# A graph layer's aggregation: one four-pass float32 product replaced by two float32r products over a split operand

## The chip, the cores and the metric

The kernel runs on one core of one Trainium2 chip. The metric is the device time of one execution in microseconds. The change is judged by the median of several runs of the changed kernel against the median of the kernel before: 936.79 us, from three runs between 936.75 and 937.58 us.

## The reference

One layer over 1250 nodes with 512 features and 20000 edges: a graph convolution, a linear attention and a two-of-four mixture of delta-rule memories. What the change touches is the graph convolution:

```python
def _L0_gnn_ref(x, W, b, edge_index):
    src = jnp.concatenate([edge_index[0], self_loops])
    dst = jnp.concatenate([edge_index[1], self_loops])
    deg = jax.ops.segment_sum(ones, dst, num_segments=N)
    dinv_sqrt = jnp.where(deg > 0, jax.lax.rsqrt(deg), 0.0)
    norm = dinv_sqrt[src] * dinv_sqrt[dst]
    h = x @ W
    msgs = h[src] * norm[:, None]
    agg = jax.ops.segment_sum(msgs, dst, num_segments=N)
    return jax.nn.relu(agg + b)
...
xn = _layernorm(x, axis=-1)
x = x + _L0_gnn_ref(xn, ...) + _L0_mix_ref(xn[None], ...)[0]
x = x + _L0_ffn_ref(_layernorm(x, axis=-1)[None], ...)[0]
```

## The kernel before, in words

Nodes are tiled by P = 125 rows, so there are NT = 10 tiles of source nodes (s) and 10 of destination nodes (t). The features are 512 = KC * 128 columns.

The kernel is a hand-ordered program: each engine has its own instruction list and they meet only at semaphores. Its stages, in time:

1. Up to about 216 us: layer norm of x, the linear attention, and a sort of the edges into bins by their source tile.
2. Up to about 307 us: the counting. The number of edges from each source node to each destination is built as a product of one-hot matrices (float16) on TensorE (L557), with VectorE making the one-hots (L1646, L1652). ScalarE copies the counts from PSUM into `big`, seen as `cnt` (L1088), and GpSimd adds the self loops (L1337). Between these products TensorE computes h = xn @ W (L690), which ScalarE copies to `hs` (L1084).
3. About 307 to 323 us: TensorE forms the last attention outputs with `mix(7)`, `mix(8)`, `mix(9)` (L571) and the degrees (L719). VectorE adds 1 to the degrees (L1714). A branch, not taken with these inputs, holds further rounds of counting for a bin that overflows (TensorE L724, VectorE L1717). GpSimd takes the power -0.5 of the degrees into `dinv` (L1339). VectorE adds the attention outputs to x (`mix_out`, L1609) and multiplies each `hs` tile by `dinv` in place (L1732).
4. About 323 to 419 us: the aggregation. For each destination tile t TensorE sums ten products `cnt[:, s, t] x hs[:, s]` over s into one PSUM bank (L770), both operands float32. Behind t = 8 and 9, and woven into them, stand token logits (L743) and the first feature projections (L754), and behind t = 5, 6, 8 and 9 transposes of normalised rows (L529). VectorE scales each result by `dinv` and adds the bias (L1740), applies the relu and adds to x (L1743), and takes the statistics of the next layer norm (L1471 to L1476); GpSimd takes the power -0.5 of the variances (L1307); VectorE normalises rows (L1484).
5. From 419 us: the mixture: gates, projections (L754), scatter of rows to DRAM by GpSimd (L1357), ten units of a chunked recurrence up to about 870 us, gather, gate, output projection (L1023).

The order around the change. TensorE runs t = 0 to 9 strictly in order; in t = 0 it waits before each s for `hs_done` (L769), and from t = 2 on it waits for the sum of t - 2 on VectorE (L766). VectorE makes all ten `hs` tiles, with `mix_out(9)` between tiles 3 and 4, before it turns to the sums. SP issues the loads of the five mixture weights once `mix(9)` is done (L415 to L418).

Of the kernel before, what the change touches and what calls it, by code (L numbers as in the profile page):

```python
# [25 lines left out]
P = 125  # L26
NT = N // P
# [71 lines left out]
def gps_layer(nc, d, out):  # L99
    f32, i32, f16, bf16 = mybir.dt.float32, mybir.dt.int32, mybir.dt.float16, mybir.dt.bfloat16  # L100
    ALU = mybir.AluOpType
# [3 lines left out]
    with ctx:  # L105
# [16 lines left out]
        xT = sb("xT", [128, KC, N + 3])  # L122

        big = sb("big", [128, NT * N])
        cnt = big[0:P, :].rearrange("p (t n) -> p t n", t=NT)
        fT = big[:, 0:2 * D].rearrange("p (k n) -> p k n", k=2)
        hs = sb("hs", [P, NT, D])
        W = sb("W", [128, 5, KC, D])
# [23 lines left out]
        xn = sb("xn", [128, 2, D])  # L152
        tA = sb("tA", [128, 2, D])
        tB = sb("tB", [128, 2, D])
        tC = sb("tC", [128, 2, D])
# [4 lines left out]
        b_q1 = sb("b_q1", [128, 2, KC])  # L160
        dinv = sb("dinv", [P, NT])
        deg = sb("deg", [P, NT])
# [196 lines left out]
        def sort_after_q(u):  # L359

            return SORT_KV * (NT - SORT_FROM) + SB * min(2 * u, 8 + u)

        def last_sum(dve, V, t):
            dve.wait_ge(S["y_psum"], t + 1)
            if t >= 2:
                dve.wait_ge(out_stored[t % 2], 32 * (t // 2))
            V.tensor_tensor(tC[0:P, t % 2, :], bank[0:P, 6 + t % 2, :], x_all[:, t, :], ALU.add).then_inc(S["y_done"], 1)
# [3 lines left out]
        def _(sp):  # L371
# [40 lines left out]
            for s in range(NT):  # L412
                sp.wait_ge(S["count_done"], 2 * s + 2)
                sp.dma_start(deg_rows[s:s + 1, :], big[P:OW, s * N:(s + 1) * N]).then_inc(S["deg_rows_loaded"], 16)
            sp.wait_ge(S["mix_psum"], NT)  # L415
# [102 lines left out]
        def _(pe):  # L518
# [205 lines left out]
            with pe.If(n_rounds > 1):  # L724
                pe.wait_ge(S["count_done"], NB)
                with pe.Fori(1, n_rounds) as r:
                    pe.wait_ge(S["count_done"], r * NB)
                    count_round(r)
                pe.wait_ge(S["counted"], 1)
                mm(bank[:, 7, 0:16], zeros16[:, 0:128], zeros16[:, 0:16], start=True, stop=True)  # L730
                for s in range(NT):
                    last = degrees(s)
                last.then_inc(S["deg_psum"], 1)

            mix(8, 5)
# [28 lines left out]
            for t in range(NT):  # L764
                if t >= 2:
                    pe.wait_ge(S["agg_sum"], t - 1)  # L766
                for s in range(NT):
                    if t == 0:
                        pe.wait_ge(S["hs_done"], s + 1)  # L769
                    last = mm(bank[0:P, t % 2, :], cnt[:, s, t * P:(t + 1) * P], hs[:, s, :], start=(s == 0), stop=(s == NT - 1))  # L770
                    if t >= 8 and 1 <= s < 9:
                        token_logits(2 * (t - 8) + (s - 1) // KC, (s - 1) % KC)
                last.then_inc(S["agg_psum"], 1)
                if t >= 8:
                    pe.wait_ge(W_loaded[t - 8], 32)
# [260 lines left out]
        def _(act):  # L1036
# [43 lines left out]
            for g in range(NB):  # L1080
# [4 lines left out]
                act.wait_ge(S["onehots_used"], (g + 1) * SC)  # L1085
                to = big[0:OW, s * N:(s + 1) * N].rearrange("p (n a) -> p n a", a=2)
                for k, (t0, n) in enumerate(HCOLS):
# [7 lines left out]
            def feature_rows(t, w):  # L1095
# [8 lines left out]
                else:  # L1104
                    A(hs[:, t, :].rearrange("p (b j e) -> p b j e", b=2, e=DH), by_halves(feature_bank(t, 3), P),
                      ACT.Silu).then_inc(S["f_act"], 1)

            copy_tiles(0, 8, NT)
            act.wait_ge(S["agg_psum"], NT)
# [186 lines left out]
        def _(pool):  # L1296
# [37 lines left out]
            for t in range(NT):  # L1334
                pool.wait_ge(S["count_done"], 2 * t + 2)
                v = cnt[:, t, t * P:(t + 1) * P]
                G.tensor_tensor(v, v, ident[0:P, 0:P], ALU.add).then_inc(S["loops_added"], 1)  # L1337
            pool.wait_ge(S["deg_final"], 1)
            G.tensor_tensor(dinv[:, :], deg[:, :], phalf[0:P, 0:NT], ALU.pow).then_inc(S["dinv_done"], 1)  # L1339
            for t in range(LB, NT):  # L1340
# [125 lines left out]
        def _(dve):  # L1466
# [250 lines left out]
            with dve.If(n_rounds > 1):  # L1717
                dve.wait_ge(S["loops_added"], NT)
                with dve.Fori(1, n_rounds) as r:
                    count_round(r)  # L1720
                V.tensor_copy(n_r, n_max).then_inc(S["counted"], 1)
                dve.wait_ge(S["deg_psum"], 2)
                V.tensor_copy(deg[:, :], bank[0:P, 7, 0:NT])
            V.tensor_copy(n_r, n_max).then_inc(S["deg_final"], 1)
            mix_out(8, 5)
            dve.wait_ge(S["dinv_done"], 1)
            for t in range(NT):
                if t == 0:
                    dve.wait_ge(S["h_done"], NT)
                if t == 4:  # L1730
                    mix_out(9, 4)
                V.tensor_scalar(hs[:, t, :], hs[:, t, :], dinv[:, t:t + 1], None, ALU.mult).then_inc(S["hs_done"], 1)  # L1732
            for t in range(NT):
# [304 lines left out]
```

## Time and profile before

| | us |
|---|---|
| median of three runs | 936.79 |
| the profiled execution | 932.14 |
| its span, first to last instruction | 930.2 |
| TensorE busy, share of the span | 92% |
| VectorE busy | 66% |
| ScalarE, GpSimd busy | 33%, 36% |
| mean granted TensorE clock | 0.987 |

The busy share of TensorE is high almost everywhere, so the share alone doesn't say what a stage is worth; the chain that ended last and the waits of each stage do. Instruction durations of TensorE include the time to drain, and one starts while the one before is still draining: the time that a stream of them takes is read from their starts, or from the pieces of the chain. A float32 matmul stands in the profile as two records of TensorE, each with a weight load (PEld) of its own: the 100 products of L770 are 200 records.

### The profile page before, as it was taken

The numbers are of one execution on the slowest core, as the hardware profiler recorded it, in microseconds if no ns is written. First come the engines' busy times: TensorE is split into PE (matmuls) and PEld (weight loads), VectorE is DVE, ScalarE is ACT, GpSimd is POOL, SyncE is SP. The second block draws the span as 40 slices with busy tenths as digits, with TensorE's granted clock in tenths as the row PEclk, the third lists the DMA queues.
The fourth block names the chain that finished last, engine by engine and source line by source line (L and its number), as shares of the span: only waits on it lengthen the run. The fifth ranks groups of instructions, "written<-read, shape, count | busy, mean of one in ns | idle before, by whom it ended". The sixth has DMA issues, their size and how long they took to land.

```text
span 930.2 us, 24269 instructions
## 1 busy us (share of the span) xinstructions
PE 854.6 (92%) x10394; PEld 551.9 (59%) x10394; DVE 618.3 (66%) x1306; ACT 305.7 (33%) x538; POOL 338.3 (36%) x300
## 2 busy tenths in 40 slices
PE   2989999999999899999799988898999999988898
PEld 2544444345666444455344436898888898888443
DVE  7999999976888323222852546776666676655295
ACT  1221112201222000002454633554554545454352
POOL 6221100000111300000274136776776777662460
PEclk9999999999999999999999999999999999999999
DMA  8500000220000060000009464454444554421462
GB/s 243 171 0 1 1 1 1 45 46 23 2 0 2 5 245 0 1 0 1 2 7 376 188 237 109 112 141 129 124 134 112 134 139 126 135 73 37 112 181 66
DMA packets 74962, 80.49 MB, mean 87 GB/s; under 512 B 34453, under 2 KB 57671, under 8 KB 74854
## 3 DMA queue, kind: packets, MB, share of 16 engines
q1 hardware_dynamic: 69733, 57.78, 22.4%
q0 software_dynamic: 5120, 21.14, 6.3%
q8 instruction: 84, 1.38, 0.6%
q14 instruction: 25, 0.20, 0.1%
HBM read 54.44 MB, written 24.39 MB: 85 GB/s over the span
## 4 chain that ended last, share of the span: by engine, by line
PE 69%; DVE 22%; issue 4%; ACT 2%; DMA 2%; POOL 1%; SPq 1%; DVEq 0%; POOLq 0%
PE bank L754 10%; PE bank L770 9%; PE bank L822 9%; PE bank L848 4%; PE bank L571 4%; PE bank L1023 4%; PE bank L557 3%; DVE rows L1517 3%; DVE rows L1646 3%; DVE rows L1519 2%; PE bank L911 2%; PE bank L924 2%; PE bank L948 2%; PE bank L839 2%; PE bank L935 2%
## 5 line engine op out<-in xcount | busy, mean ns | idle before, releaser
L754 PE MATMUL bank<-W,xT 128*128 128x512 f32 x272 | 123.7, 608 | 4.8 <-ACT big L1100 4.8
L754 PEld LDWEIGHTS bank<-W,xT 128*128 128x128 f32 x272 | 51.6, 194 | 65.2 <-issue 59.2
L770 PE MATMUL bank<-hs,big 125*125 125x512 f32 x200 | 90.0, 599 | 0.0
L535 PE MATMUL bank<-W,xT 128*125 128x512 f32 x160 | 78.2, 603 | 0.0
L1337 POOL TENSOR_TENSOR big<-big,ident_sb 125x125 f32<-125x125 f32 x10 | 11.4, 1142 | 173.8 <-ACT big L1088 173.8
L557 PEld LDWEIGHTS bank<-rows 128*126 128x126 f16 x360 | 43.5, 135 | 34.7 <-issue 24.2
L1652 DVE TENSOR_SCALAR rows<-iota_sb,tC 128x625 f16<-128x625 f16 x180 | 56.2, 378 | 10.5 <-PE bank L557 10.5
L557 PE MATMUL bank<-rows 128*126 128x313 f16 x360 | 58.9, 299 | 4.2 <-DVE rows L1652 4.1
L770 PEld LDWEIGHTS bank<-hs,big 125*125 125x125 f32 x200 | 36.1, 188 | 39.1 <-issue 38.9
L1517 DVE TENSOR_SCALAR rows<-iota_sb,gbp 125x180 f16<-125x180 f16 x160 | 56.2, 351 | 0.0
L1042 ACT ACTIVATE xT<-bank 128x500 f32<-128x500 f32 x20 | 11.0, 588 | 133.6 <-PE bank L529 133.6
L1740 DVE SCALAR_TENSOR_TENSOR tA<-bank,dinv,b_g 125x512 f32<-125x512 f32 x10 | 7.5, 751 | 66.2 <-PE bank L770 66.2
L1519 DVE TENSOR_SCALAR rows<-iota_sb,gbp 125x180 f16<-125x180 f16 x160 | 50.4, 315 | 0.0
L1307 POOL TENSOR_TENSOR rstd<-mv,phalf 125x5 f32<-125x5 f32 (+2 forms) x5 | 5.3, 1068 | 117.6 <-DVE mv L1476 117.6
L545 PE MATMUL bank<-rows 125*128 125x360 f16 x160 | 42.5, 320 | 5.1 <-DVE rows L1519 3.3
L822 PE MATMUL bank<-big 64*64 64x64 f32 (+1 forms) x1280 | 43.4, 212 | 2.7 <-issue 1.9
L535 PEld LDWEIGHTS bank<-W,xT 128*125 128x125 f32 x160 | 29.4, 193 | 25.9 <-issue 25.3
L1185 ACT ACTIVATE tB<-bank 128x1024 f16<-128x1024 f32 x40 | 40.8, 1021 | 8.9 <-PE bank L876 8.8
L624 PE MATMUL bank<-xT,W 128*128 128x500 f32 (+1 forms) x96 | 42.1, 520 | 1.3 <-ACT W L1077 0.7
L948 PE MATMUL bank<-state,W 64*64 64x64 f32 x640 | 41.7, 222 | 1.1 <-issue 0.9
L822 PEld LDWEIGHTS bank<-big 64*64 64x64 f32 (+1 forms) x1280 | 39.0, 128 | 3.7 <-issue 3.1
L952 PE MATMUL bank<-tC,W 64*64 64x64 f32 x640 | 40.4, 218 | 0.6 <-issue 0.6
(334 smaller groups left out, 1974.5 us busy)
## 6 DMA issues: line engine op xcount, KB each, us to landing
big<-qkv_slots SPq DMA_DIRECT2D x40, 256.0 KB, 3.7
rows<-step_rows SPq DMA_DIRECT2D x40, 128.0 KB, 3.1
rows<-gam_rows SPq DMA_DIRECT2D x40, 128.0 KB
big<-qkv_slots SPq DMA_DIRECT2D x80, 64.0 KB, 2.8
big<-qkv_slots SPq DMA_DIRECT2D x40, 128.0 KB, 3.0
o_slots<-big SPq DMA_DIRECT2D x40, 128.0 KB, 2.9
x_all<-in_x SPq DMA_DIRECT2D x10, 224.0 KB
out<-tC SPq DMA_DIRECT2D x10, 224.0 KB
```

The lines of the kernel that those rows point to most:

```text
L535: last = mm(dst, xT[:, k, t * P:(t + 1) * P], W[:, w, k, :], start=(k == 0), stop=(k == KC - 1 and bias is None))
L545: mm(bank[:, 7, 0:2 * SW], oh_row[:, i // SB % SR, i % SB, :], oh_col[:, i % (SR * SB), :, :].rearrange("p a n -> p (a n)"), start=False, ...
L557: last = mm(bank[0:OW, b0 + k, 0:n], oh_src[:, g % 2, j, :], oh_dst[:, i % WB, t0:t0 + n], start=(j == 0), stop=(j == SC - 1))
L624: last = mm(bank[:, u % 2, 0:n], W[:, 2, k, c * 128:(c + 1) * 128], xT[:, k, t0:t0 + n], start=(k == 0), stop=(k == KC - 1))
L754: last = mm(bank[:, b0, :], xT[:, k, t * P:t * P + 128], W[:, w, k, :], start=(k == 0), stop=(k == KC - 1))
L770: last = mm(bank[0:P, t % 2, :], cnt[:, s, t * P:(t + 1) * P], hs[:, s, :], start=(s == 0), stop=(s == NT - 1))
L822: last = mm(bank[q, b0, a * CL:(a + 1) * CL], lhsT[q, a, :], rhs[q, a, :], start=start(a), stop=True, skip_group_check=not start(1))
L948: mm(bank[q, DB, o0 + j * DH:o0 + (j + 1) * DH], qG[u // 2 % 2][u % 2][q, c2 * HB + j, :], state[q, c % 2, j, :], start=True, stop=False)
L1185: A(TM[s].rearrange("p (z a) w n -> p z (a w n)", z=2), bank[:, TB[s]:TTB[s] + 1, :], ACT.Copy).then_inc(S["tm_done"], 1)
L1517: V.tensor_scalar(oh_col[:, i % (SR * SB), 0, :], iota[0:P, 0:SW], e_col[:, i:i + 1], e_src[:, i:i + 1], ALU.is_equal, ALU.mult)
L1519: V.tensor_scalar(oh_col[:, i % (SR * SB), 1, :], iota[0:P, 0:SW], e_col[:, i:i + 1], e_dst[:, i:i + 1], ALU.is_equal, ALU.mult).then_inc( ...
L1652: V.tensor_scalar(oh_dst[:, i % WB, :], iota[:, 0:HN], srt[:, 1, i:i + 1], None, ALU.is_equal).then_inc(S["onehots_done"], 1)
```

## The change

The counts are stored as float32r, a 4-byte type that the change takes to keep 12 significant bits; a count is a small integer and stays as it is. The scaled rows `hs * dinv` are split into two float32r parts: `hs_high`, the scaled row rounded to float32r, written by ScalarE, and `hs_low`, the scaled row minus `hs_high`, written by VectorE over the memory of `hs`. Each product of L770 becomes two matmuls with both operands float32r, one for each part, added into the same PSUM bank.

- L1732, ten one-operand multiplications on VectorE, goes. In its place ScalarE does ten copies with a scale read from `dsrc` (a second copy of `dinv`), and VectorE ten `scalar_tensor_tensor` that each wait for its high part.
- ScalarE waits for `mix_done` 9, `dinv_done` 1 and `h_done` NT before the first of them, since `hs_high` lies over `tB`, `tC` and the one-hot rows.
- The power on GpSimd takes 20 values instead of 10 per partition.
- In the branch that isn't taken there is now an aggregation in float32 of its own, for counts after further rounds.
- The degree rows' DMA, the self loops and the count copies now address the same bytes as float32r.

```diff
+        with nc.sbuf_tensor("cnt_r", [128, NT * N], f32r) as cnt_r:
+            pass
         big = sb("big", [128, NT * N])
         cnt = big[0:P, :].rearrange("p (t n) -> p t n", t=NT)
+        cnt12 = cnt_r[0:P, :].rearrange("p (t n) -> p t n", t=NT)
...
+        with nc.sbuf_tensor("hs_r", [P, NT, D], f32r) as hs_low:
+            pass
         hs = sb("hs", [P, NT, D])
...
-        dinv = sb("dinv", [P, NT])
+        dinv2 = sb("dinv", [P, 2, NT])
+        dinv, dsrc = (dinv2[:, n, :] for n in range(2))
...
@@ TensorE, inside pe.If(n_rounds > 1)
+                pe.wait_ge(S["counted"], 3)
+                for t in range(NT):
+                    if t >= 2:
+                        pe.wait_ge(S["counted"], 2 + t)
+                    for s in range(NT):
+                        last = mm(bank[0:P, t % 2, :], cnt[:, s, t * P:(t + 1) * P], hs[:, s, :], start=(s == 0), stop=(s == NT - 1))
+                    last.then_inc(S["deg_psum"], 1)
...
@@ TensorE, the aggregation
-                    last = mm(bank[0:P, t % 2, :], cnt[:, s, t * P:(t + 1) * P], hs[:, s, :], start=(s == 0), stop=(s == NT - 1))
+                    mm(bank[0:P, t % 2, :], cnt12[:, s, t * P:(t + 1) * P], hs_high[:, s, :], start=(s == 0), stop=False)
+                    last = mm(bank[0:P, t % 2, :], cnt12[:, s, t * P:(t + 1) * P], hs_low[:, s, :], start=False, stop=(s == NT - 1))
...
@@ ScalarE
-                to = big[0:OW, s * N:(s + 1) * N].rearrange("p (n a) -> p n a", a=2)
+                to = cnt_r[0:OW, s * N:(s + 1) * N].rearrange("p (n a) -> p n a", a=2)
...
+            act.wait_ge(S["mix_done"], 9)
+            act.wait_ge(S["dinv_done"], 1)
+            act.wait_ge(S["h_done"], NT)
+            for t in range(NT):
+                A(hs_high[:, t, :], hs[:, t, :], ACT.Copy, scale=dsrc[:, t:t + 1]).then_inc(S["h_done"], 1)
             copy_tiles(0, 8, NT)
...
@@ GpSimd
-            G.tensor_tensor(dinv[:, :], deg[:, :], phalf[0:P, 0:NT], ALU.pow).then_inc(S["dinv_done"], 1)
+            G.tensor_tensor(dinv2[:, :, :], bm(deg[:, :], 2), bm(phalf[0:P, 0:NT], 2), ALU.pow).then_inc(S["dinv_done"], 1)
...
@@ VectorE
             for t in range(NT):
-                if t == 0:
-                    dve.wait_ge(S["h_done"], NT)
                 if t == 4:
                     mix_out(9, 4)
-                V.tensor_scalar(hs[:, t, :], hs[:, t, :], dinv[:, t:t + 1], None, ALU.mult).then_inc(S["hs_done"], 1)
+                dve.wait_ge(S["h_done"], NT + t + 1)
+                V.scalar_tensor_tensor(hs_low[:, t, :], hs[:, t, :], dsrc[:, t:t + 1], hs_high[:, t, :],
+                                       ALU.mult, ALU.subtract).then_inc(S["hs_done"], 1)
```

VectorE's part of the branch that isn't taken (a copy of the counts to float32 ahead of the rounds, the scaling, ten copies of the results, and counts replaced by an identity) is left out here.

## Rows read from the trace of the kernel before

**Rows 1.** The page, part 4: the chain that ended last, by engine.
```profile
PE 69%; DVE 22%; issue 4%; ACT 2%; DMA 2%; POOL 1%; SPq 1%; DVEq 0%; POOLq 0%
```

**Rows 2.** Busy time of each engine by stretch: aggregation, and one ahead.
```profile
core 0: us, PE busy (x) PEld busy (x) DVE busy (x) ACT busy (x) POOL busy (x), PEclk, DMA share, GB/s
323.40:423.00 99.60, 99.60 (x277) 46.77 (x275) 32.04 (x60) 3.20 (x6) 4.16 (x4) 1.00 0.16 58
...
315.24:318.70 3.46, 3.46 (x5) 1.51 (x6) 0.00 (x0) 0.00 (x0) 3.46 (x3) 0.53 0.03 7
```

**Rows 3.** The chain in order of time, aggregation (start us, us, what).
```profile
323.98 51.50 PE bank L770 x120
...
376.34 8.59 PE bank L770 x20
...
419.34 3.44 PE bank L754 x8
```

**Rows 4.** Groups by line and form, TensorE: busy us, mean ns | idle before.
```profile
L770 PE MATMUL bank<-hs,big 125*125 125x512 f32 x200 | 90.0, 599 | 0.0
L557 PE MATMUL bank<-rows 128*126 128x313 f16 x180 | 50.8, 301 | 4.2 <-DVE rows L1652 4.1
...
L540 PE MATMUL bank<-big 96*125 96x512 bf16 x10 | 3.8, 380 | 0.0
```

**Rows 5.** Timeline of TensorE, 94.9 to 95.2 us (start us, us, instruction).
```profile
94.94 0.38 PE L540 MATMUL bank<-big 96*125 96x512 bf16 x1
95.16 1.02 PE L535 MATMUL bank<-W,xT 128*125 128x512 f32 x2
```

**Rows 6.** The chain just ahead of the aggregation.
```profile
310.63 2.27 PE bank L719 x20
312.90 2.34 issue
315.24 8.74 PE bank L571 x16
```

**Rows 7.** Timeline of VectorE, 320 to 335 us.
```profile
320.59 0.69 DVE L1609 TENSOR_TENSOR x_all<-bank,x_all 125x512 f32<-125x512 f32 x1 [5.79 <-PE bank L571]
321.19 2.68 DVE L1732 TENSOR_SCALAR hs<-hs,dinv 125x512 f32<-125x512 f32 x4
324.02 0.69 DVE L1609 TENSOR_TENSOR x_all<-bank,x_all 125x512 f32<-125x512 f32 x1
324.63 3.47 DVE L1732 TENSOR_SCALAR hs<-hs,dinv 125x512 f32<-125x512 f32 x6
...
333.39 0.69 DVE L1743 SCALAR_TENSOR_TENSOR x_all<-tA,x_all 125x512 f32<-125x512 f32 x1
334.12 0.69 DVE L1471 BATCH_NORM_STATS2 stats<-x_all 125x6 f32<-125x512 f32 x1
```

**Rows 8.** Groups by line and form, ScalarE: SBUF copies, with and without scale operand.
```profile
L1253 ACT ACTIVATE big<-big,c_t 125x512 f32<-125x512 f32 x10 | 7.1, 710 | 2.6 <-DMA big<-o_slots,posi 2.6
L1257 ACT ACTIVATE big<-big 125x512 f32<-125x512 f32 x10 | 6.3, 630 | 6.0 <-DVE big L1973 5.7 <-issue 0.3
```

**Rows 9.** Timeline of GpSimd at 315 us.
```profile
314.88 1.97 POOL L1339 TENSOR_TENSOR dinv<-deg,phalf 125x10 f32<-125x10 f32 x1 [6.16 <-DVE t L1724]
```

**Rows 10.** The last mixture weight: its issue, and us from issue to landing.
```profile
326.49 2.31 SPq L418 DMA_DIRECT2D W<-in_L_ffn_Wo  x1
...
W<-in_L_ffn_Wo SPq DMA_DIRECT2D x1, 1024.0 KB, 15.5
```

**Rows 11.** Timeline of the second normalisation, around t = 7 and t = 8.
```profile
394.47 0.75 DVE L1740 SCALAR_TENSOR_TENSOR tA<-bank,dinv,b_g 125x512 f32<-125x512 f32 x1 [7.30 <-PE bank L770]
...
397.83 1.01 POOL L1307 TENSOR_TENSOR rstd<-mv,phalf 125x4 f32<-125x4 f32 x1 [35.03 <-DVE mv L1476]
...
404.75 0.75 DVE L1740 SCALAR_TENSOR_TENSOR tA<-bank,dinv,b_g 125x512 f32<-125x512 f32 x1 [7.00 <-PE bank L770]
...
406.99 1.00 DVE L1484 TENSOR_SCALAR xn<-x_all,mv,rstd 125x512 f32<-125x512 f32 x2
```

More of the change, by code:

```diff
@@ L99, in gps_layer @@
 def gps_layer(nc, d, out):
-    f32, i32, f16, bf16 = mybir.dt.float32, mybir.dt.int32, mybir.dt.float16, mybir.dt.bfloat16
+    f32, i32, f16, bf16, f32r = mybir.dt.float32, mybir.dt.int32, mybir.dt.float16, mybir.dt.bfloat16, mybir.dt.float32r
     ALU = mybir.AluOpType
@@ L153, in gps_layer @@
         tA = sb("tA", [128, 2, D])
+        with nc.sbuf_tensor("hs_high", [P, NT, D], f32r) as hs_high:
+            pass
         tB = sb("tB", [128, 2, D])
@@ L361, in sort_after_q, with aggregated @@
             return SORT_KV * (NT - SORT_FROM) + SB * min(2 * u, 8 + u)
+        def aggregated(t):
+            return rows_all[0:P, (t - 4) * D:(t - 3) * D] if t >= 4 else (tB, tC)[t // 2][0:P, t % 2, :]
         def last_sum(dve, V, t):
@@ L413, in _ @@
                 sp.wait_ge(S["count_done"], 2 * s + 2)
-                sp.dma_start(deg_rows[s:s + 1, :], big[P:OW, s * N:(s + 1) * N]).then_inc(S["deg_rows_loaded"], 16)
+                sp.dma_start(deg_rows[s:s + 1, :], cnt_r[P:OW, s * N:(s + 1) * N].bitcast(f32)).then_inc(S["deg_rows_loaded"], 16)
             sp.wait_ge(S["mix_psum"], NT)
@@ L728, in _ @@
                     count_round(r)
-                pe.wait_ge(S["counted"], 1)
+                pe.wait_ge(S["counted"], 2)
                 mm(bank[:, 7, 0:16], zeros16[:, 0:128], zeros16[:, 0:16], start=True, stop=True)
@@ L1335, in _ @@
                 pool.wait_ge(S["count_done"], 2 * t + 2)
-                v = cnt[:, t, t * P:(t + 1) * P]
+                v = cnt12[:, t, t * P:(t + 1) * P]
                 G.tensor_tensor(v, v, ident[0:P, 0:P], ALU.add).then_inc(S["loops_added"], 1)
             pool.wait_ge(S["deg_final"], 1)
-            G.tensor_tensor(dinv[:, :], deg[:, :], phalf[0:P, 0:NT], ALU.pow).then_inc(S["dinv_done"], 1)
+            G.tensor_tensor(dinv2[:, :, :], bm(deg[:, :], 2), bm(phalf[0:P, 0:NT], 2), ALU.pow).then_inc(S["dinv_done"], 1)
             for t in range(LB, NT):
@@ L1718, in _ @@
                 dve.wait_ge(S["loops_added"], NT)
+                for t in range(NT):
+                    last = V.tensor_copy(cnt[:, t, :], cnt12[:, t, :])
+                last.then_inc(S["counted"], 1)
+                dve.wait_ge(S["counted"], 1)
                 with dve.Fori(1, n_rounds) as r:
@@ L1722, in _ @@
                 dve.wait_ge(S["deg_psum"], 2)
-                V.tensor_copy(deg[:, :], bank[0:P, 7, 0:NT])
+                V.tensor_copy(deg[:, :], bank[0:P, 7, 0:NT]).then_inc(S["deg_final"], 1)
+                dve.wait_ge(S["h_done"], NT)
+                dve.wait_ge(S["dinv_done"], 1)
+                for t in range(NT):
+                    last = V.tensor_scalar(hs[:, t, :], hs[:, t, :], dinv[:, t:t + 1], None, ALU.mult)
+                last.then_inc(S["counted"], 1)
+                for t in range(NT):
+                    dve.wait_ge(S["deg_psum"], 3 + t)
+                    V.tensor_copy(aggregated(t), bank[0:P, t % 2, :]).then_inc(S["counted"], 1)
+                dve.wait_ge(S["counted"], 3 + NT)
+                V.memset(dsrc, 1.0)
+                for t in range(NT):
+                    V.tensor_copy(hs[:, t, :], aggregated(t))
+                    last = V.tensor_scalar(cnt12[:, t, :], cnt[:, t, :], 0.0, None, ALU.mult)
+                last.then_inc(S["counted"], 1)
+                dve.wait_ge(S["counted"], 4 + NT)
+                for t in range(NT):
+                    last = V.tensor_copy(cnt12[:, t, t * P:(t + 1) * P], ident[0:P, 0:P])
+                last.then_inc(S["counted"], 1)
+                dve.wait_ge(S["counted"], 5 + NT)
             V.tensor_copy(n_r, n_max).then_inc(S["deg_final"], 1)
```

## The prediction

> **What bounds the kernel now.** I read the share of each engine in the chain that ended last first: TensorE holds 69% of it, VectorE 22% [rows 1]. Then the stretch of the aggregation: from 323.4 to 423 us TensorE is busy for all of its 99.6 us, VectorE for 32.0, ScalarE for 3.2, and the granted clock is 1.00, which is the 2.4 GHz level [rows 2]. So here TensorE alone sets the pace, and a microsecond less on it is a microsecond less of the span, as long as nobody else becomes late. Third, the chain in order of time gives the price of a record: 120 records of L770 in 51.50 us, 20 in 8.59 us, so 0.4295 us each, 0.859 us for one float32 product, and 200 x 0.4295 = 85.9 us for the aggregation [rows 3]. The stretch from 323.98 to 419.34 us is 95.4 us [rows 3]; the other 9.5 are logits, transposes and one projection, which the change leaves alone. The mean of 599 ns for a record [rows 4] is not the price: it includes the drain, which overlaps.
>
> **Term 1, the products.** Removed are 200 records of 0.4295 us; added are 200 matmuls (10 x 10 x 2) with 512 moving columns each. No float32r matmul stands in this trace, so its price has to be bounded. What does the 0.4295 consist of? A float16 record with 313 columns lasts 301 ns on average, the bfloat16 one with 512 columns 380 ns, and the float32 one with 512 columns 599 ns [rows 4]. From 313 to 512 columns of 16-bit data: 79 ns for 199 columns, 0.4 ns a column, one column per cycle at 2.4 GHz. From there to float32: 219 ns more for the same 512 columns, so a float32 record streams them twice, and a product, being two records, four times. A single pass of 512 columns is then half a record, 0.4295 / 2 = 0.215 us. It can also be seen whole: the bfloat16 matmul starts at 94.94 us and the next matmul, a float32 one, at 95.16 us, 0.22 us behind it [rows 5], with its own weight load and a change of type on both sides at no extra price. If float32r is one pass, it costs 0.215 to 0.22 us. I take 0.216, so 200 x 0.216 = 43.2 us, and the term is 43.2 - 85.9 = -42.7 us.
>
> The nearest rows for its bounds: the bottom is the single pass (0.215), since nothing in the trace takes less per column. The top is a record as it is now (0.4295), or even two of those (0.859), if float32r were treated like float32. I stay at the bottom end: four streamings are what two halves by two halves need (my reading of the four, not a row), the operands handed over here are such halves already, and 16-bit operands, which need no splitting, are streamed once [rows 4]. What each of these ends costs is priced under the rivals.
>
> The Trainium skill, page "FP8 and Floating Point Precision", section "TensorE Precision Notes", says that the array works natively at about FP22, that "FP32 reduced precision" reads 4-byte words and truncates them, and that true float32 takes four passes. The rows above agree on the four passes; that the reduced form takes one is shown by no row here. By the page the term would be the same -42.7 us; by the row of float32 taken as it is, 0.
>
> **The weight loads.** There are 200 before and 200 after, but each now has 0.216 us of matmul to hide behind instead of 0.43. The 20 records of L719, with 125 weight columns of float32 and one moving column, take 2.27 us: 0.114 us each [rows 6], and that is all weight load. 0.114 is below 0.216, and loads run ahead of the matmul now (the float32 stream has no idle time before it [rows 4]), so they cost nothing. If they stopped running ahead, each would cost 0.114 (a rival, below).
>
> The Trainium skill, page "TensorE: Matmul & The Clock Gate", section "Weight-path perf modes — Fast Weight Load (FWL) and DoubleRow", speaks against the change on one point: the fast load is for 128 weights and not for FP32. Here there are 125 weights, so it would be out with any type, and the sum stays as it is with or without that rule; the measured 0.114 us is what counts.
>
> **Term 2, the start.** Before, VectorE made the ten tiles in 2.68 + 3.47 us with `mix_out(9)` between [rows 7], and the first s were ready before TensorE came to them. Now the tile passes ScalarE and then VectorE. ScalarE may start when `mix_out(8)` is done, at 320.59 + 0.69 = 321.28 us [rows 7]. A copy with a scale operand, SBUF to SBUF, takes 0.71 us [rows 8] (0.63 without the operand is the lower bound). VectorE's two-operand instruction takes 0.69 us, and 0.73 from start to start with a wait between (333.39 to 334.12) [rows 7]. So: first high part at 322.0, low parts 0 to 3 from 322.1 to 325.0, `mix_out(9)` to 325.7, low parts 4 to 9 at 0.73 to 330.1 (ScalarE is ahead by then: its tenth ends at 321.3 + 7.1 = 328.4). TensorE needs its last pair behind that, 0.43, so t = 0 ends at about 330.6 us. Unhindered it would end at 323.98 + 20 x 0.216 = 328.3. The loss is 2.3 us, once; bounds 1.5 (if the waits cost nothing) and, below, 4.5. TensorE's own start isn't held up: the first low part is there at 322.8, before 323.98. What waits behind these instructions: on ScalarE nothing until the transposes behind t = 5; on VectorE the sum of t = 0, which needs TensorE's end of t = 0 anyway.
>
> The short stops of TensorE in t = 0, some 0.3 us between pairs, might let the clock fall. The trace has one such fall: after 2.34 us without work the next matmuls ran at a granted 0.53, the 1.2 GHz level [rows 2, 6]. Stops here are much shorter, and I count nothing; the bound is t = 0 at half rate, 20 x 0.43 = 8.6 us instead of 6.6, 2.0 to 2.2 us more.
>
> **The rest at nothing.** The power over 20 values: 1.97 us for 10, ending at 316.85 [rows 9]; even twice that ends at 318.8, ahead of the 321.28 that `mix_out(8)` sets anyway; that cover is 2.4 us. The count copies, self loops and the degree DMA move the same bytes. The jump over a longer branch: 2.34 us of "issue" today [rows 6]; the jump is made already, a longer target may add some tenths of a microsecond, at most 1; I take 0.
>
> **Who could be late in a faster aggregation.** A tile takes 20 x 0.216 = 4.3 us instead of 8.6. VectorE does 32.0 us of work in this stretch [rows 2], of it 6.2 for the scaling; the rest is under 3 us per tile, below 4.3. Second, the normalisation: the first transposes stand two tiles behind their rows. For t = 7 the chain is 394.47 to 397.83 + 1.01 us, 4.4 us [rows 11]; its result is wanted behind t = 8 (4.3 + eight logits, about 6 us). The transposes behind t = 8 follow a projection of 3.44 us [rows 3], while VectorE has the first of them ready 2.7 us after its sum starts (404.75 to 407.5) [rows 11]; both sides of that race stay as they are. Third, the weights: the last is issued at 326.49 and takes 15.5 us, landed by 342 [rows 10]; the first use is behind t = 8, now at about 368 us. So the aggregation ends at 419.34 - 42.7 + 2.3 = 378.9 us, and everything behind it starts from what it produced, so it moves by the same amount.
>
> **The sum.** -42.7 + 2.3 = -40.4 us. Against the profiled execution: 932.14 - 40.4 = 891.7 us. The median of the runs is 936.79, 4.65 above that execution, so 891.7 + 4.65 = 896.4 us.
>
> **Rivals.**
> - Loads that no longer hide: 200 x 0.114 = 22.8 us on top, less the 2.3 us of the start that then vanish in a slower t = 0: 896.4 + 20.5 = 917 us. For it: the room to hide halves. Against: 0.114 fits in 0.216, and the bfloat16 pass at 0.22 [rows 5] hid its load. 5%.
> - Float32r streams a column every two cycles, as a float32 record does: 200 x 0.4295, no gain; the scaling's 0.73 per tile is then below the 0.859 of a pair, so the start costs nothing either: 937 us, within 0.2%. For it: 4-byte operands are never read faster in this trace. 4%.
> - Slower than before: the chip, or what the program is turned into, carries out a float32r matmul as a full float32 product of two records. Each costs 0.859, 400 records instead of 200, +85.9 us: 1022.7 us. It decides from a price above 0.43 us per matmul. This would also be the case in which the change doesn't do what it says. For it: nothing in the trace; against: the operands' types differ from before. 4%.
> - My forecast, single pass with hidden loads: 87%. Within it the price may be up to 0.24 (200 x 0.024 = +4.8 us), the start up to +2.2, the jump +1; downwards -0.8 at the start and up to 4.65 if the gap between profile and median closes.
>
> **Range and chances.** 891 to 904 us holds the forecast with most of its bounds, some 8 in 10. A measurement of this kernel can tell about 0.2%, 1.9 us, from no change. Faster 0.92 (the forecast and the first rival), same 0.04, slower 0.04.
>
> **What would show it.** 200 records for the new products, of 380 ns, as the bfloat16 one now, at 0.216 us from start to start; the last record of t = 0 behind VectorE's tenth low part near 330.6 us, VectorE's list full from 322 to 330; the first projection of tile 1 behind t = 9 not at 419.34 but at 379; no new wait at L766 or the transposes; the stages behind unchanged in length. Records of 590 ns, or 400 of them, would make the prediction wrong at its first term; starts 0.33 us apart would point to the loads.

## The result: 898.98 us, and the profile after

The changed kernel takes 898.98 us in the median of four runs (897.02 to 901.04), the kernel before 936.88 us beside it. The ratio is 0.961, with an interval of 0.959 to 0.964: faster by 3.9%, 37.9 us. The prediction was 896.4 us with a range of 891 to 904. In a later set of runs one execution of the changed kernel took 1360.62 us at a mean granted clock of 0.56; it is in none of the numbers below.

The profiled execution took 899.98 us, with a span of 897.7. Its chain by engine looks as before [rows 1]: a stage was shortened, and TensorE still sets the end.

```profile
PE 67%; DVE 23%; issue 4%; DMA 2%; ACT 2%; POOL 1%; SPq 1%; DVEq 0%; POOLq 0%
```

The chain in order of time, around the aggregation (start us, us, what), answers [rows 3] and [rows 6]. L582 is `mix(8)` and `mix(9)`, L788 and L789 are the two new products, L772 is the projection that stood in L754.

```profile
312.78 2.19 issue
314.97 6.47 PE bank L582 x8
321.47 0.70 DVE x_all L1633
322.19 0.73 ACT hs_high L1131
323.02 3.03 DVE hs_r L1778 x4
326.05 0.60 DVE x_all L1633
326.65 2.36 DVE hs_r L1778 x2
...
332.42 0.23 PE bank L788
...
355.60 0.85 PE bank L540 x8
...
383.66 3.44 PE bank L772 x8
```

The aggregation now ends at 383.66 us, against 419.34. A new piece stands ahead of it: `mix_out(8)`, ScalarE's first high part, VectorE's low parts. Tiles 1 to 5, 100 matmuls, run without a stop from 332.42 to the transposes (L540) at 355.60: 0.232 us from one start to the next. The groups by line and form of this stretch answer [rows 4]:

```profile
L788 PE MATMUL bank<-hs_high,cnt_r 125*125 125x512 f32 x100 | 42.0, 420 | 1.5 <-DVE hs_r L1778 1.5
L789 PE MATMUL bank<-hs_r,cnt_r 125*125 125x512 f32 x100 | 39.4, 394 | 0.0
```

There are 200 records, one for each float32r matmul, of some 393 ns each (median of L789) where a float32 record took 592 and the bfloat16 one 380. One pass, then, but at 0.232 us from start to start not quite the 0.22 of the 16-bit one. The timeline of VectorE and GpSimd in tile 0 answers [rows 7]:

```profile
323.02 3.03 DVE L1778 SCALAR_TENSOR_TENSOR hs_r<-hs,dinv,hs_high 125x512 fp32r<-125x512 f32 x4 [0.86 <-ACT hs_high L1131]
...
325.97 0.68 DVE L1633 TENSOR_TENSOR x_all<-bank,x_all 125x512 f32<-125x512 f32 x1
...
326.57 5.07 DVE L1778 SCALAR_TENSOR_TENSOR hs_r<-hs,dinv,hs_high 125x512 fp32r<-125x512 f32 x6
326.73 1.72 POOL L1334 TENSOR_TENSOR x_all<-x_all,tA 125x512 f32<-125x512 f32 x1 [3.22 <-DVE x_all L1633]
...
332.46 0.75 DVE L1787 SCALAR_TENSOR_TENSOR tA<-bank,dinv,b_g 125x512 f32<-125x512 f32 x1 [0.82 <-PE bank L789]
```

The first four low parts take 3.03 us, the last six 5.07: the price of a low part is not constant. Ten of them with nothing beside them would take 0.66 us each and 0.08 more at the end of a group. The last six are 1.0 us above that, all of it in one low part of 1.76 us that stands beside GpSimd's addition at 326.73; the first four are 0.3 us above it, beside an addition that ends at 323.51 (322.24, 1.27 us). The sum of tile 0, which waits for TensorE's end of it, starts at 332.46 us; the prediction had 330.6.

Where the profiled execution stands, in us, against the prediction's own steps:

| | before | forecast | after | miss |
|---|---|---|---|---|
| `mix(8)` and `mix(9)` | 8.74 | 8.74 | 9.89 | +1.15 |
| their start | 315.24 | 315.24 | 314.97 | -0.27 |
| tile 0 | 8.6 | 6.6 | 7.6 | +1.0 |
| rest of the aggregation | 86.7 | 48.3 | 51.2 | +2.9 |
| from its end to the end of the span | 510.9 | 510.9 | 514.0 | +3.1 |
| span | 930.2 | 889.8 | 897.7 | +7.9 |

Tile 0 after is 332.46 less 324.86, the end of L582. Three questions follow. Why is a float32r matmul dearer than 0.216 us? What happens in tile 0? And did the change cause the 3.1 us behind the aggregation and the 1.15 ahead of it, or do executions differ by so much?

### The profile page after: what moved, and what is told of

Same layout as the page of the kernel before. It is cut to its first block, busy times and chain, and to the rows that moved or that the text cites. A ratio compares the mean times of both kernels' runs of the same rounds, so it can differ in the third digit from the quotient of the medians.

```text
span 897.7 us, 24280 instructions
## 1 busy us (share of the span) xinstructions
PE 818.5 (91%) x10394; PEld 552.7 (62%) x10394; DVE 618.5 (69%) x1306; ACT 311.9 (35%) x548; POOL 338.8 (38%) x300
## 4 chain that ended last, share of the span: by engine, by line
PE 67%; DVE 23%; issue 4%; DMA 2%; ACT 2%; POOL 1%; SPq 1%; DVEq 0%; POOLq 0%
PE bank L772 10%; PE bank L841 10%; PE bank L867 5%; PE bank L1042 4%; PE bank L582 4%; DVE rows L1541 4%; PE bank L568 4%; DVE rows L1543 3%; PE bank L788 3%; DVE rows L1670 3%; PE bank L930 2%; PE bank L789 2%; PE bank L858 2%; PE bank L943 2%; PE bank L967 2%
## 5 line engine op out<-in xcount | busy, mean ns | idle before, releaser
L772 PE MATMUL bank<-W,xT 128*128 128x512 f32 x272 | 123.8, 608 | 4.8 <-ACT big L1119 4.8
L772 PEld LDWEIGHTS bank<-W,xT 128*128 128x128 f32 x272 | 51.6, 194 | 64.5 <-issue 57.9
L546 PE MATMUL bank<-W,xT 128*125 128x512 f32 x160 | 77.8, 600 | 0.0
L1361 POOL TENSOR_TENSOR cnt_r<-cnt_r,ident_sb 125x125 fp32r<-125x125 f32 x10 | 11.4, 1142 | 173.8 <-ACT cnt_r L1107 173.8
L788 PE MATMUL bank<-hs_high,cnt_r 125*125 125x512 f32 x100 | 42.0, 420 | 1.5 <-DVE hs_r L1778 1.5
L1962 DVE TENSOR_TENSOR big<-bank,masks_sb 128x512 f16<-128x512 f32 x40 | 27.5, 688 | 22.2 <-PE bank L841 22.2
L1962 DVE TENSOR_TENSOR tA<-bank,masks_sb 128x512 f16<-128x512 f32 x40 | 27.5, 687 | 22.0 <-PE bank L841 22.0
L556 PEld LDWEIGHTS bank<-rows 125*128 125x128 f16 x160 | 15.5, 97 | 42.8 <-DVE rows L1543 27.5
L701 PE MATMUL bank<-W,xT 128*125 128x512 f32 x80 | 40.8, 591 | 0.0
```

Source lines behind the costliest of these rows:

```text
L546: last = mm(dst, xT[:, k, t * P:(t + 1) * P], W[:, w, k, :], start=(k == 0), stop=(k == KC - 1 and bias is None))
L556: mm(bank[:, 7, 0:2 * SW], oh_row[:, i // SB % SR, i % SB, :], oh_col[:, i % (SR * SB), :, :].rearrange("p a n -> p (a n)"), start=False, ...
L772: last = mm(bank[:, b0, :], xT[:, k, t * P:t * P + 128], W[:, w, k, :], start=(k == 0), stop=(k == KC - 1))
L788: mm(bank[0:P, t % 2, :], cnt12[:, s, t * P:(t + 1) * P], hs_high[:, s, :], start=(s == 0), stop=False)
L1962: V.tensor_tensor(B16[lv % 2][s], pm(MB[s]), bm(level[lv], 8), ALU.mult).then_inc(S["b_done"], 1)
```

## The experiments

Each had the kernel before timed beside it on the same chip, whose median lay between 931.4 and 934.9 us; so ratios are compared, not microseconds of different chips.

### Does the change cost something outside its stage?

The kernel before, unchanged:

> The kernel before, unchanged, for a second profile of it. Theory A (the 3.3 us that the changed kernel lost behind the aggregation are the variation from one execution to the next): the stretch from the end of the aggregation to the end of the span, 510.9 us in the first profile, comes out one to five us longer here, since the median of the runs lies 4.65 above the first profile, and the nine float32 matmuls ahead of the aggregation that ran at half clock in the changed kernel (against four in the first profile) may be four or eight here. Theory B (the change itself costs them): 511 us again within 0.5, and four half-rate records again.

The changed kernel, unchanged, four times in all:

> The changed kernel, unchanged, timed more often and profiled again. The ratio stays 0.961 within 0.002. Theory A: the stretch behind the aggregation (514.0 us in its first profile) varies by a microsecond or more. Theory B: 514.0 again within 0.5. The pitch of the float32r matmuls is 0.232 us again in both.

> The changed kernel a third time, for one more profile beside those of the same chip. The stretch behind the aggregation between 510 and 516 us, half-rate records of mix(8) and mix(9) four, seven or another number, if these vary by execution.

> The changed kernel again, timed in the same rounds as the two others, so that their ratios can be set against it on one chip. 0.963 of the kernel before, within 0.003; tile 0 ends at about 332.2 with one low part of 1.76 us.

> The changed kernel beside it: 0.963 of the kernel before within 0.003; the matmuls of mix(8) and mix(9) take between 8.7 and 9.9 us, as in the profiles so far, whatever the kernel.

The kernel before came out at 1.0015 of itself (0.9991 to 1.0039), the changed one at 0.9658, 0.9629 and 0.9589 in three sets of rounds (each to about 0.003 either way); the kernel of the third expectation ran once, 900.79 us, beside 934.49 of the kernel before. Two of the expectations on the ratio missed: 0.9658 was expected within 0.002 of 0.961, and 0.9589 within 0.003 of 0.963. The first and the last of these sets lie 0.7% apart, more than their intervals, so ratios of different sets are not compared below. From the profiles of both kernels, in us; the last column is the span less the start of the last product:

| profile | `mix(8)`, `mix(9)` | last product starts | span | behind it |
|---|---|---|---|---|
| before, first | 8.74 | 418.8 | 930.2 | 511.4 |
| before, again | 9.74 | 420.2 | 935.3 | 515.1 |
| changed, first | 9.89 | 383.3 | 897.7 | 514.4 |
| changed, again | 9.84 | 383.4 | 897.3 | 513.9 |
| changed, third | 8.83 | 384.0 | 898.6 | 514.6 |
| changed, fourth | 8.66 | 383.7 | 891.6 | 507.9 |
| changed, fifth | 9.82 | 383.5 | 893.2 | 509.7 |

The kernel before varies behind the aggregation by 3.7 us, the changed one by 6.7, and their ranges overlap. The second profile of the changed kernel alone (513.9 after 514.4) would still have fitted theory B; the second of the kernel before (515.1) and the fourth of the changed one (507.9) decide for theory A: 3.1 us between two profiles is no more than executions differ by. The first profile of before lay at the short end, as its distance of 4.65 us from the median suggested. The same with the 1.15 us ahead: 8.74 is four float32 records at half clock in 16, 9.74 and 9.89 are six to seven ((9.89 - 0.16 - 16 x 0.4295) / 0.4295 = 6.7, with 0.16 us of drain). Both kernels show both. My expectation for this column, nine half-rate matmuls, was a miscount.

One thing the expectations did not have: in the third and the fourth profile the clock fell again, in tile 0. Busy time by stretch, of the fourth profile and then of the second:

```profile
core 0: us, PE busy (x) PEld busy (x) DVE busy (x) ACT busy (x) POOL busy (x), PEclk, DMA share, GB/s
323.90:333.00 9.10, 7.43 (x22) 4.45 (x22) 7.61 (x11) 3.56 (x6) 1.74 (x2) 0.81 0.81 294
```

```profile
323.90:333.00 9.10, 7.62 (x26) 4.07 (x25) 8.28 (x12) 4.65 (x8) 1.72 (x1) 1.00 0.72 254
```

And the timeline of TensorE in the fourth:

```profile
330.24 0.63 PE L789 MATMUL bank<-hs_r,cnt_r 125*125 125x512 f32 x1
330.67 0.63 PE L788 MATMUL bank<-hs_high,cnt_r 125*125 125x512 f32 x1
```

A granted clock of 0.81 over the stretch, and float32r matmuls 0.43 us apart where the full clock gives 0.23: the 1.2 GHz level, after TensorE had stopped several times for a low part, and until 332 us. Tile 0 then takes 9.0 us (332.88 less 323.88) instead of 7.6, but that isn't the price of the clock. These are just the profiles in which the clock came back early ahead of the aggregation (8.83 and 8.66), so TensorE began tile 0 earlier, while VectorE's tenth low part was done at 331.4 in both, against 331.6 in the first profile: its first four low parts began 0.6 and 1.0 us earlier but took 3.41 and 3.76 us instead of 3.03, with more of GpSimd's additions beside them. From the tenth low part to the sum of tile 0 it took 1.8 and 1.5 us instead of 0.8. So the low clock cost 1.0 and 0.7 us, and tile 0 ends at 332.5 to 333.2 us either way.

### What a float32r matmul costs

> The changed kernel with seven streams of 40 matmuls put ahead of the aggregation, each from start to start, into a PSUM bank nobody reads: float32r 125 weights x 512, x 384 and x 256 columns; 64 weights x 512; 128 weights x 512; float16 125 weights x 512; float32 125 weights x 512. The question is where 0.232 - 0.2133 = 0.019 us of a float32r matmul comes from. Theory F (a fixed price for each matmul): 384 and 256 columns give 0.160 + 0.019 = 0.179 and 0.107 + 0.019 = 0.126, and the weights' number doesn't matter. Theory L (a part of the weight load that is not hidden): as F in the columns, but 64 weights give less, about 0.223 or less, and 128 a bit more. Theory C (4-byte columns stream slower): 0.232 / 512 per column, so 0.174 and 0.116, whatever the weights. Float16 tells whether the price is the type's: 0.216 if it is float32r's alone, 0.232 if every single-pass matmul pays it. Float32: 0.859. The streams add 40 x (0.232 + 0.179 + 0.126 + 0.232 + 0.232 + 0.22 + 0.859) = 83 us to the time, less up to 4 us, since the split is done before TensorE comes to tile 0: 978 to 982 us.

```diff
             pe.wait_ge(S["small_loaded"], 64)
+            pe.wait_ge(S["count_done"], NB)
+            pe.wait_ge(S["hs_done"], NT)
+            for n in range(40):
+                mm(bank[0:P, 2, :], cnt12[:, n % NT, n * 16:n * 16 + P], hs_high[:, n % NT, :], start=True, stop=True)
...
             for t in range(NT):
```

The chain of that kernel; the seven streams stand in the order of the expectation:

```profile
333.14 11.43 PE bank L786 x40
344.57 7.00 PE bank L788 x40
351.57 4.71 PE bank L790 x40
356.29 9.23 PE bank L792 x40
365.52 9.29 PE bank L794 x40
374.80 8.63 PE bank L796 x40
383.43 34.33 PE bank L798 x80
```

The kernel took 988.45 us in one execution, above the 978 to 982 expected: TensorE stood still for 7.5 us before the first stream, which then began at the low clock (11.43 us for what 40 times 0.232 puts at 9.3) and isn't used; its place takes the 0.232 of the aggregation. 384 columns: 7.00 / 40 = 0.175 us. 256 columns: 0.118. So 128 columns cost 0.0573 us, 0.447 ns each, and with 0.232 at 512 the step from 384 is the same again. 512 x 0.447 is 229 ns; some 3 ns are left of 232. The surplus is in the columns, not in the matmul. 64 weights cost 0.231, 128 weights 0.232: it isn't the load. Float16, with 125 weights and 512 columns, costs 0.216 and float32 0.858. Theory C holds, F and L fall: a float32r column streams 7% slower than a 16-bit one (0.447 against (0.2158 - 0.003) / 512 = 0.416 ns, if the float16 matmul has the same 3 ns, which no second length shows). The float16 stream multiplied zeros. That this isn't what makes it cheap, the changed kernel's own float16 matmuls of the counting show: eight with 312 or 313 columns start within 1.08 us (304.71 to 305.79), 0.135 each, where 0.447 ns a column would give 0.143. A float32 pass doesn't show this (0.858 / 4 = 0.2145). Why 4-byte operands in a single pass are slower isn't shown here. The timeline of TensorE in the changed kernel:

```profile
304.71 1.24 PE L568 MATMUL bank<-rows 128*126 128x313 f16 x8
305.79 1.02 PE L701 MATMUL bank<-W,xT 128*125 128x512 f32 x2
```

### Is TensorE still what the aggregation waits for?

> The low part's 100 matmuls are left out of the aggregation (the split on ScalarE and VectorE still makes both parts), so the result lacks the low bits. If TensorE sets the pace of the aggregation at 0.232 us for each float32r matmul: tiles 1 to 9 lose 90 x 0.232 = 20.9 us, and tile 0, which waits for VectorE, some 0.2: about 21 us faster than the changed kernel, 878 us. Rival: with 2.3 us of products for a tile instead of 4.6, VectorE's sums and statistics (about 2.3 us a tile with their waits) become the pace: 16 to 19 us faster, with TensorE waiting for the sum of two tiles before.

```diff
-                    mm(bank[0:P, t % 2, :], cnt12[:, s, t * P:(t + 1) * P], hs_high[:, s, :], start=(s == 0), stop=False)
-                    last = mm(bank[0:P, t % 2, :], cnt12[:, s, t * P:(t + 1) * P], hs_low[:, s, :], start=False, stop=(s == NT - 1))
+                    last = mm(bank[0:P, t % 2, :], cnt12[:, s, t * P:(t + 1) * P], hs_high[:, s, :], start=(s == 0), stop=(s == NT - 1))
```

883.24 us, 0.9457 (0.9419 to 0.9495), against 900.73 (the median of its five executions) and 0.9658 of the changed kernel in the same rounds: 17.5 us less, where 20.9 us of matmuls went. In the two profiles the last product starts 17.7 us earlier (365.7 against 383.4). That is the size the rival expected, but its mechanism explains only half of what is missing. From VectorE's list, TensorE's, and the busy time by stretch (columns as in the stretches above, 0.50 is PEclk):

```profile
338.82 0.75 DVE L1786 SCALAR_TENSOR_TENSOR tA<-bank,dinv,b_g 125x512 f32<-125x512 f32 x1
...
341.13 0.75 DVE L1786 SCALAR_TENSOR_TENSOR tA<-bank,dinv,b_g 125x512 f32<-125x512 f32 x1
```

```profile
331.78 13.88 PE L788 MATMUL bank<-hs_high,cnt_r 125*125 125x512 f32 x52 [0.17 <-DVE hs_r L1777]
347.15 1.10 PE L540 MATMUL bank<-ident_sb,xn 125*128 125x125 f32 x8 [1.50 <-DVE xn L1507]
```

```profile
331.80:334.00 2.20, 2.20 (x5) 1.52 (x6) 1.32 (x2) 0.00 (x0) 0.00 (x0) 0.50 1.01 378
```

From tile 1 on TensorE runs 52 matmuls without a stop: it is still the pace, and 2.31 us from one tile's sum to the next is its time for ten matmuls, which VectorE's list nearly fills. They take some 1.6 us more than 52 times 0.232, because the clock was at the 1.2 GHz level (0.50) when they began. Only then, behind tile 5, does TensorE wait 1.5 us for a normalised row, which VectorE has late because its list is now as long as TensorE's. So VectorE would be about to become the pace at half of the products. With both it isn't: a tile takes 4.6 us, and VectorE waited 26.9 us for L789 in the changed kernel.

### What holds tile 0

Four edits, from the smallest. First `mix_out(9)` behind the tenth low part, which also moves GpSimd's addition to that tile out of the split:

> mix_out(9) moved from between the fourth and fifth low part to behind the tenth. Theory: in tile 0 TensorE waits for VectorE's list (four low parts 3.03 us, mix_out 0.6, six low parts 5.07 us, of which the first two took 2.4 us beside GpSimd's addition of the bias to the same tile). Without mix_out in the list and without GpSimd beside it, ten low parts take 7.6 us from 323.0 to 330.6 instead of 331.6: the aggregation ends about 1.0 us earlier, up to 1.6 if GpSimd was what slowed them; the ratio to the changed kernel 0.998 to 0.999. Rival (the slow low parts come from something else than GpSimd): 0.6 us, and single low parts of 0.8 us and more remain.

```diff
             for t in range(NT):
-                if t == 4:
-                    mix_out(9, 4)
                 dve.wait_ge(S["h_done"], NT + t + 1)
...
+            mix_out(9, 4)
```

The timeline of VectorE:

```profile
323.50 7.00 DVE L1776 SCALAR_TENSOR_TENSOR hs_r<-hs,dinv,hs_high 125x512 fp32r<-125x512 f32 x10 [0.86 <-ACT hs_high L1131]
```

Ten low parts in 7.00 us. Tile 0 takes 6.0 us (331.32 less 325.34), 1.6 less than the 7.6 of the changed kernel: the theory's upper figure. The time is 0.9598 (0.9574 to 0.9622); the changed kernel ran only once in these rounds, so the times don't tell the two apart.

Second, GpSimd alone:

> The changed kernel with one edit: GpSimd adds the bias to tiles 5 to 9 of x only when all ten low parts are done; mix_out(9) stays between low parts 3 and 4. It isolates GpSimd from the length of VectorE's list. Theory: no low part over 0.8 us; the ten low parts and mix_out(9) end at about 330.6 instead of 331.6 (start 323.0, ten at 0.66 and one at 0.6, plus 0.1), so the aggregation ends 1.0 us earlier. Rival: a low part of 1.7 us remains behind mix_out(9), without GpSimd beside it, and nothing changes.

```diff
+            pool.wait_ge(S["hs_done"], NT)
             for t in range(LB, NT):
                 pool.wait_ge(S["mix_done"], t + 1)
                 add_bias(t)
```

The durations of the low part's line, min, median and max in ns, in the changed kernel and in this one:

```profile
L1778 DVE SCALAR_TENSOR_TENSOR hs_r<-hs,dinv,hs_high x10: 735/740/1764, 323.0 to 330.9; 125x512 fp32r<-125x512 f32 x10
```

```profile
L1779 DVE SCALAR_TENSOR_TENSOR hs_r<-hs,dinv,hs_high x10: 742/746/752, 323.8 to 330.3; 125x512 fp32r<-125x512 f32 x10
```

And the timeline of TensorE and VectorE:

```profile
315.47 10.13 PE L582 MATMUL bank<-W,xn 128*125 128x512 f32 x16 [2.20 <-issue]
...
327.02 4.06 DVE L1779 SCALAR_TENSOR_TENSOR hs_r<-hs,dinv,hs_high 125x512 fp32r<-125x512 f32 x6
```

The one low part of 1764 ns is gone, with `mix_out(9)` still in its place. VectorE's list, from the first low part to the end of the tenth, takes 7.3 us (323.76 to 331.08) instead of 8.6 (323.02 to 331.64), and tile 0 takes 6.3 us (331.90 less 325.60), 1.3 less. In the experiment before, the list took 7.0 us: of its 1.6 us, 0.6 are `mix_out(9)` in the list and 1.0 is GpSimd's addition beside the last six low parts. This one removes the 0.3 us beside the first four as well. The time is 892.97 us, 0.9603 (0.9565 to 0.9640), against 0.9629 of the changed kernel in the same rounds: the intervals overlap.

Third, ScalarE and VectorE start as soon as the scales are there:

> ScalarE no longer waits for mix_out(8) but for the end of VectorE's branch and the power on GpSimd, and VectorE makes low parts 0 to 3 before mix_out(8), 4 to 6 before mix_out(9), the others behind it. Theory (what the start costs is the late release of ScalarE by mix_out(8), at 322.19 us, while the scales are ready at 318.3): the high parts start at 318.4, the low parts at 319.2 and are done by about 328.5, as TensorE needs them: tile 0 takes 4.7 us instead of 8.0, 3.3 us faster than the changed kernel, about 895.5 us. Rival (GpSimd's additions of the bias, now beside more of the low parts, slow VectorE): 1 to 2 us only, with low parts of 1 us and more.

```diff
+            V.tensor_copy(small[:, 77:78], n_max).then_inc(S["split_ok"], 1)
-            mix_out(8, 5)
             dve.wait_ge(S["dinv_done"], 1)
             for t in range(NT):
                 if t == 4:
+                    mix_out(8, 5)
+                if t == 7:
                     mix_out(9, 4)
...
-            act.wait_ge(S["mix_done"], 9)
+            act.wait_ge(S["split_ok"], 1)
```

It gains nothing that the times show: 900.75 us, 0.9644 (0.9624 to 0.9664), and tile 0 takes 7.6 us as before. The low parts start 4.2 us earlier than in the changed kernel's first profile and end only 0.7 us earlier (331.0 against 331.6). The durations of their line:

```profile
L1780 DVE SCALAR_TENSOR_TENSOR hs_r<-hs,dinv,hs_high x10: 736/811/1778, 318.8 to 330.2; 125x512 fp32r<-125x512 f32 x10
```

The timeline of GpSimd and VectorE at their head:

```profile
317.89 4.63 POOL L1334 TENSOR_TENSOR x_all<-x_all,tA 125x512 f32<-125x512 f32 x3
...
318.83 4.91 DVE L1780 SCALAR_TENSOR_TENSOR hs_r<-hs,dinv,hs_high 125x512 fp32r<-125x512 f32 x4 [4.47 <-ACT hs_high L1131]
```

Four low parts take 4.91 us instead of 2.7, three additions 4.63 instead of 3.71. The two engines hold each other up, and the time won is spent on that. The rival was right, and with its 1 to 2 us it was still too hopeful.

Fourth, the early start with GpSimd held back, that is with the two `split_ok` lines of the third edit:

> The early split (ScalarE released by the end of VectorE's branch and the power) with GpSimd's additions of the bias held back until all ten low parts are done, mix_out(8) between low parts 4 and 5, mix_out(9) behind the tenth. Theory (what ate the gain of the early split was GpSimd beside VectorE: single low parts of 1.76 us instead of 0.74): low parts start at 318.9 and take 0.66 us from start to start, the tenth is done at about 326.5, before TensorE needs it, so tile 0 takes 4.7 us as every other tile: 3.3 us faster than the changed kernel on the same chip (ratio to it 0.996), with no wait of TensorE for a low part. Rival (something else slows the low parts): the tenth comes after 328.5 and TensorE waits in tile 0 as before.

> The early split with GpSimd held back, timed once more beside the changed kernel, because executions of one kernel differ by up to 1% on this chip and the gain of 3.0 us that its trace shows is 0.3%. Theory: the ratio to the changed kernel of the same rounds is 0.996 to 0.998 again. Rival: what tile 0 gains is given back behind the aggregation, where GpSimd's held-back additions run beside VectorE's first sums: ratio 1.000, with the stretch from the end of the aggregation to the end 3 us longer.

```diff
             for t in range(NT):
-                if t == 4:
-                    mix_out(9, 4)
+                if t == 5:
+                    mix_out(8, 5)
...
+            mix_out(9, 4)
...
+            pool.wait_ge(S["hs_done"], NT)
```

The durations of the low part's line, and the timeline of VectorE behind them:

```profile
L1779 DVE SCALAR_TENSOR_TENSOR hs_r<-hs,dinv,hs_high x10: 741/746/752, 319.3 to 325.8; 125x512 fp32r<-125x512 f32 x10
```

```profile
329.64 0.75 DVE L1789 SCALAR_TENSOR_TENSOR tA<-bank,dinv,b_g 125x512 f32<-125x512 f32 x1 [2.46 <-PE bank L789]
330.42 1.83 DVE L1792 SCALAR_TENSOR_TENSOR x_all<-tA,x_all 125x512 f32<-125x512 f32 x1
```

The tenth low part is done at 326.6 us, tile 0 takes 4.7 us (329.64 less 324.98) like any other, and the last product starts at 380.5 in both profiles, against 383.7 and 383.5 in the changed kernel of the same rounds: 3.2 and 3.0 us, as expected. GpSimd now meets VectorE's first sums (1.83 us for one that takes 0.69 alone), but these have room. Behind the last product the two pairs of profiles disagree: 513.4 us against 507.9 in the first, 509.3 against 509.7 in the second. All four lie within the 507.9 to 514.6 of the five profiles of the changed kernel, so nothing shows that the gain is given back there, and only the second pair speaks directly against it. The times: 0.9589 (0.9549 to 0.9628) and 0.9573 (0.954 to 0.9607), against 0.9629 and 0.9589 of the changed kernel in the same rounds; medians 893.57 and 895.82 against 896.23 and 897.14 us. Both are on the side of a gain, of 2.7 and 1.3 us; the intervals overlap, so the gain is shown by the traces up to the last product and only suggested by the times. By the traces it is the best version run here; by the times the second edit, GpSimd alone, is not told apart from it.

## Why the prediction was right, step by step

**What bounds the stage**: right. TensorE was the pace, and leaving out half of the new products took away 17.5 of 20.9 us, half of the rest going to the low clock.

**Term 1, the products**: right in kind, 7% too low in price. One record for each matmul and one stream of the columns: so the prediction's likeliest case, and none of the three rivals. 0.216 was taken from half a float32 record and from the bfloat16 matmul at 0.22 [rows 3, 5]. Neither of the two is a 4-byte operand streamed once, and that is the case that costs 0.232. 200 x 0.016 = 3.2 us, of which 2.9 fall on tiles 1 to 9. The row to price it from didn't exist in that trace; the bound of 0.24 that the range took in did hold it.

**The weight loads**: right. 64, 125 and 128 weights cost the same, and a load stays hidden behind 0.232 us.

**Term 2, the start**: mechanism right, size off: 2.3 us forecast against some 3.0, the 7.6 us of tile 0 less the 4.64 of an unhindered one. What was off is the price of a low part. The prediction took 0.73 us for each from an instruction beside which GpSimd did nothing. Alone a low part even takes 0.66 from start to start; beside GpSimd one takes 1.76. Five of the six behind `mix_out(9)` were no dearer than planned. The lower bound of 1.5 us for this loss doesn't come out of its own rows either: with 0.69 in place of 0.73 us for each low part it would be 1.9. The trace of before had the hint, in the rows that the prediction used for the old scaling: four took 2.68 us and six 3.47 [rows 7], although the median one lasts 0.476 us, and GpSimd was adding the bias beside both:

```profile
L1732 DVE TENSOR_SCALAR hs<-hs,dinv x10: 473/476/1494, 321.2 to 327.6; 125x512 f32<-125x512 f32 x10
```

```profile
321.36 1.44 POOL L1310 TENSOR_TENSOR x_all<-x_all,tA 125x512 f32<-125x512 f32 x1 [0.83 <-DVE x_all L1609]
...
324.79 1.44 POOL L1310 TENSOR_TENSOR x_all<-x_all,tA 125x512 f32<-125x512 f32 x1 [2.00 <-DVE x_all L1609]
```

The longest of the ten lasts 1494 ns: 1.0 us more, as with the low part.

The Trainium skill, page "SBUF — State Buffer", section "SBUF: two separate sides", says that VectorE with two SBUF inputs and a GpSimd operation that reads SBUF lock each other out for a whole instruction. The traces agree: a low part takes 1.76 us beside GpSimd's addition and 0.75 at most where the addition is held back. The prediction didn't weigh that rule. The delay itself isn't new with the second input, since the old scaling, with one input, had it too. What is new is that it counts: a float32 product gave VectorE 0.859 us for each tile of `hs`, the two float32r matmuls give it 0.464.

**The clock in tile 0**: the prediction counted nothing and kept 2.0 to 2.2 us as a bound. In two of five profiles of the changed kernel the clock did fall there, at a price of 1.0 and 0.7 us. In the profile compared above it didn't: that the term of nothing fits is in part luck.

**What was costed at nothing**: right. The power over 20 values took 3.54 us instead of 1.97 (314.77 to 318.3), inside its cover until 321.5. The jump over the longer branch took 2.19 us against 2.34 [rows 6]. The transposes, the second normalisation and the weights brought no new wait.

**The sum**: the aggregation was forecast to be 40.4 us shorter and was 36.6 (58.8 against 95.4); the profiled execution came out 8.3 us above its own forecast, and about half of that is one execution against another. The step to the median, adding the 4.65 us by which the first profile lay below it, was what kept the forecast of the median within 2.6 us. Part of that closeness is luck: the stage lost 3.8 us against its forecast (36.6 against 40.4), and the median only 2.5 (37.9 against 40.4), the other 1.3 us being within what executions differ by.

## What to carry to other kernels

An operand split into two parts that fit one pass turns four streams of the columns into two: the gain is nearly half of TensorE's time for these products (46.4 us in place of 85.9 here), less what the splitting costs on the other engines before the first product can run. Look for that cost at the head of the stage, where nothing hides it, and for an engine that shares a path with the one that does the splitting: starting 4.2 us earlier gained 0.7 us until GpSimd was kept away. Before a difference of a few microseconds between two profiles is explained, profile the unchanged kernel again.

## What the runs showed of the hardware

- A float32r matmul with 125 weights and 512 columns takes 0.232 us from start to start, a float16 one 0.216, a float32 one 0.858. By the differences between 256, 384 and 512 columns a float32r column costs 0.447 ns; a 16-bit one costs at most 0.421 (0.2158 / 512).
- VectorE's two-input instruction and GpSimd's two-input addition, both on 125 x 512 float32 in SBUF, don't run side by side: 0.74 us becomes 1.76 and 1.27 becomes 1.72. The same addition beside VectorE's scaling with one SBUF tensor: 0.476 us becomes 1.494.
- The clock can fall to the 1.2 GHz level while TensorE has stops of a third of a microsecond to one microsecond between pairs of matmuls: in two of five profiles of one kernel, and not in the others. It cost 0.7 and 1.0 us.
- Executions of one kernel on one chip differ by up to 7.9 us with no change in the code (the kernel before, 929.47 to 937.36 us in 17 executions). Two profiles of the changed kernel on one chip differ by 6.0 us behind the aggregation (513.9 and 507.9).
